# Softmax attention in a fused model kernel: 128-row score matmuls on masked operands become 32-row matmuls on slices of the transposed q and k, and the pipeline is cut into half units

## What is computed

```python
x_norm = layer_norm(x, g1, beta1)                       # inside, x is itself layer-normed once more
q, k, v = (x_norm @ W + b).reshape(B, S, H, hd)...      # B 2, S 1024, H 16, hd 8
q, k = apply_rope(q), apply_rope(k)
q = q * (1.0 / sqrt(hd))
scores = einsum('bhqd,bhkd->bhqk', q, k)
attn = softmax(scores, axis=-1)
out = einsum('bhqk,bhkd->bhqd', attn, v)
x = x + out @ Wo + bo
x = x + relu(layer_norm(x, g2, beta2) @ W1 + b1) @ W2 + b2
```

## Time and profile before

| | |
|---|---|
| median of 3 runs | 1262.15 us (1261.19 to 1263.75) |
| profiled execution, first to last instruction | 1262.4 us |
| first ring fill / first score / end of the last wave | 441.1 / 482.0 / 904.2 us |
| PE, DVE, ACT busy, share of the span | 75%, 55%, 40% |
| mean granted TensorE clock | 0.855 of full speed |

### The profile page before, as it was taken

One profiled execution on the slowest core, in us unless ns is written; L12 is line 12 of the kernel. 1 busy time (PEld: TensorE's weight loads), 2 busy tenths in 40 slices (PEclk: granted clock), 3 DMA queues, 4 the chain that ended last, 5 costly groups with the idle time before them and its releaser, 6 DMA issues.

```text
span 1262.4 us, 18479 instructions
## 1 busy us (share of the span) xinstructions
PE 947.6 (75%) x5666; PEld 520.6 (41%) x5666; DVE 693.4 (55%) x1340; ACT 506.2 (40%) x1039; POOL 250.6 (20%) x222
## 2 busy tenths in 40 slices
PE   4697637888455388899999999997877388585784
PEld 3376436666343312222222222221456366374563
DVE  6845774111379698777777777771243611466111
ACT  1110423333241604666666666666533133211332
POOL 1000043655206100000000000100020355201553
PEclk9799757988766757999999999999987588695898
DMA  6000110111300000000000000000021111101113
GB/s 174 21 1 1 67 34 23 41 41 41 88 1 0 18 17 9 1 17 17 2 17 2 17 17 0 9 1 1 8 60 67 42 41 39 44 1 34 34 41 91
DMA packets 39014, 37.12 MB, mean 29 GB/s; under 512 B 7922, under 2 KB 29762, under 8 KB 38946
## 3 DMA queue, kind: packets, MB, share of 16 engines
q1 hardware_dynamic: 33506, 25.02, 7.2%
q0 software_dynamic: 5440, 11.15, 3.3%
HBM read 22.18 MB, written 9.76 MB: 25 GB/s over the span
## 4 chain that ended last, share of the span: by engine, by line
PE 47%; DVE 22%; issue 10%; POOL 7%; ACT 4%; another core or an unknown queue 4%; DMA 3%; SPq 2%; ACTq 0%; DVEq 0%; POOLq 0%
PE psum L1333 10%; PE psum L1305 10%; PE psum L1261 7%; DVE arena L1272 6%; POOL results L887 4%; POOL arena L879 3%; DVE stats L158 2%; ACT arena L1365 2%; PE psum L912 2%; PE psum L217 2%; PE psum L930 2%; DVE xn L186 1%; PE psum L315 1%; PE psum L300 1%
## 5 line engine op out<-in xcount | busy, mean ns | idle before, releaser
L1272 DVE TENSOR_REDUCE arena<-psum 128x1 f32<-128x1024 f32 x256 | 302.6, 1221 | 93.5 <-PE psum L1261 92.2
L1365 ACT ACTIVATE arena<-psum 128x512 f32<-128x512 f32 x512 | 282.0, 595 | 179.0 <-PE psum L1333 177.7
L1261 PE MATMUL psum<-arena 128*128 128x512 f16 (+1 forms) x512 | 198.8, 411 | 14.7 <-DVE arena L1272 10.0
L1333 PE MATMUL psum<-arena 128*128 128x512 f16 x512 | 196.8, 389 | 14.5 <-ACT arena L1365 7.5
L1014 ACT ACTIVATE arena<-psum,e_b 128x128 f32<-128x128 f32 x340 | 96.4, 369 | 158.6 <-remote 127.5
L1333 PEld LDWEIGHTS psum<-arena 128*128 128x128 f16 x512 | 48.2, 97 | 221.3 <-ACT arena L1365 197.7
L1141 DVE TENSOR_TENSOR arena<-psum,arena 128x128 f32 (+1 forms) x85 | 24.8, 292 | 202.6 <-remote 149.5
L1305 PE MATMUL psum<-arena 128*32 128x512 f32 x1024 | 134.7, 604 | 0.0
L966 PE MATMUL psum<-arena,expert_w 128*128 128x128 f16 x1020 | 101.6, 240 | 33.3 <-ACT arena L1014 30.4
L977 PE MATMUL psum<-expert_w,arena 128*128 x680 | 105.7, 302 | 1.3 <-issue 0.7
L887 POOL DMA_INDIRECT results<-arena x85 | 83.6, 984 | 93.5 <-DVE arena L1141 78.0
(11 more groups left out here) (249 smaller groups left out, 1131.4 us busy)
## 6 DMA issues: line engine op xcount, KB each, us to landing
arena<-results SPq DMA_DIRECT2D x16, 256.0 KB, 3.8
arena<-arena SPq DMA_DIRECT2D x64, 64.0 KB, 2.0
tokens<-arena SPq DMA_DIRECT2D x6, 512.0 KB, 3.2
arena<-in_L_attn_b_w_dram SPq DMA_DIRECT2D x1, 2048.0 KB, 9.0
arena<-in_L_ffn_W_dram SPq DMA_DIRECT2D x1, 2048.0 KB, 8.8
arena<-tokens,arena POOLq DMA_INDIRECT x85
results<-arena POOLq DMA_INDIRECT x85
x<-in_L_attn_a_x_dram SPq DMA_DIRECT2D x2, 512.0 KB, 5.0
```

The lines of the kernel that those rows point to most:

```text
L1261: last = nc.tensor.matmul(core.psum[:, 2 * slot + half, :], self.qM[:, b, j, qt * P:(qt + 1) * P], keys, start=True, stop=True)
L1272: v.reduce_max(self.mx[:, qt, j:j + 1], core.psum[:, 2 * slot:2 * slot + 2, :].rearrange("p a n -> p (a n)"), AX.X).then_inc(self.ring_out, 1)
L1333: nc.tensor.matmul(core.psum[:, 4 + j % 2, :], self.kM[:, b, j, kt * P:(kt + 1) * P], self.qT2[:, b, 512 * half:512 * (half + 1)], start=True,
L1365: nc.scalar.activation(self.prob[:, k % 2, j, :], core.psum[:, 4 + j % 2, :], ACT.Exp).then_inc(self.prob_in, 1)
```

## The change

- `qM`, `kM`, their memsets, their 64 DMAs and POOL's value copies are gone. A fill takes 32 rows of `qT` as the stationary and 32 rows of `kT` as the moving operand; a score takes 32 rows of `kT` and of `qT2`. Head j uses rows 32j to 32j+31.
- DVE writes the projected values straight into `vs`, which now holds all heads of all tokens.
- The padding columns, `m4` and the ones are written by six ACT copies (`clear_pads`: 2048, 256, 1792, 1024, 256 and 5888 elements in each partition) between the roots of batch 0 and batch 1, and no longer by POOL. L1635's additions follow POOL's L1610 at once.
- The unit becomes a half unit of 512 queries; there are 16 (`HALVES`), unrolled. The first ring holds 17 positions. In `position`, the turn of half h stands between the second and the third fill of half h+2's maxima, no longer right behind its own last maximum. PE keeps two positions ahead of the turn (`AHEAD`).
- Scores use three banks (4, 5, 6) in rotation, `prob` has three buffers; the wave sums in bank 7 alone, and ACT, no longer DVE, copies the sum, once for each half.
- One period on PE is now: two scores, a fill (both matmuls of one head), two scores, the rest of the fills (one; in the last period of a half two, one turn among the three of that period), the wave of the period before.

```diff
-ARENA = 28608
+ARENA = 29184
...
+    HALVES = 2 * B * NG
+    POSITIONS = 17 * HALVES
+    AHEAD = 2
+    SCORE_BANKS = 3
+    PROBS = 3
...
+    def position(a):
+        if a < 17:
+            return ("turn", 0, 0) if a == 16 else ("max", 0, a)
+        if a < 33:
+            return "max", 1, a - 17
+        h, i = divmod(a - 33, 17)
+        h += 2
+        if h == SoftmaxAttention.HALVES:
+            return "turn", h - 1, 0
+        if i == 2:
+            return "turn", h - 1, 0
+        return "max", h, i - (i > 2)
...
+    def turn_at(h):
+        return 16 if h == 0 else SoftmaxAttention.POSITIONS - 1 if h == SoftmaxAttention.HALVES - 1 else 18 + 17 * h
...
     def ring_fill(self, pe, a):
+        if a >= 2:
+            pe.wait_ge(self.ring_out, a - 1)
...
-        last = nc.tensor.matmul(core.psum[:, 2 * slot + half, :], self.qM[:, b, j, qt * P:(qt + 1) * P], keys,
-                                start=True, stop=True)
+        rows = slice(32 * j, 32 * j + 32)
+        for keys in range(2):
+            k0 = b * S + 512 * keys
+            last = nc.tensor.matmul(core.psum[:, 2 * slot + keys, :], self.qT[rows, g, q0:q0 + P],
+                                    self.kT[rows, g, k0:k0 + 512], start=True, stop=True)
...
+    def score(self, pe, k, j):
+        tile = HG * k + j
+        if tile >= self.SCORE_BANKS:
+            pe.wait_ge(self.prob_in, tile - self.SCORE_BANKS + 1)
+        rows = slice(32 * j, 32 * j + 32)
+        at = b * S + kt * P
+        nc.tensor.matmul(core.psum[:, 4 + tile % self.SCORE_BANKS, :], self.kT[rows, g, at:at + P],
+                         self.qT2[rows, h % 2, :], start=True, stop=True).then_inc(self.score_in, 1)
...
     def wave(self, pe, k):
+        pe.wait_ge(self.prob_in, HG * k + HG)
+        if kt == 0 and h:
+            pe.wait_ge(self.sum_out, h)
         for j in range(HG):
+            last = nc.tensor.matmul(core.psum[32 * j:32 * j + 32, 7, :], self.vs[:, b * TB + kt, HG * g + j, :],
+                                    self.prob[:, k % self.PROBS, j, :], start=(kt == 0), stop=(kt == TB - 1))
...
+    def loop_tensor(self, pe):
+        a = 0
+        waves = TB * self.HALVES
+        for k in range(waves):
+            h, kt = divmod(k, TB)
+            upto = min(self.POSITIONS, self.turn_at(h) + 1 + self.AHEAD + (17 * kt) // TB)
+            if k == 0:
+                while a < upto:
+                    self.ring_fill(pe, a)
+                    a += 1
+            after = min(self.POSITIONS, self.turn_at(h) + 1 + self.AHEAD + (17 * (kt + 1)) // TB)
+            if kt == 0:
+                pe.wait_ge(self.ring_out, self.turn_at(h) + 1)
+            self.score(pe, k, 0)
+            self.score(pe, k, 1)
+            if a < after:
+                self.ring_fill(pe, a)
+                a += 1
+            self.score(pe, k, 2)
+            self.score(pe, k, 3)
+            while a < after:
+                self.ring_fill(pe, a)
+                a += 1
+            if k > 0:
+                self.wave(pe, k - 1)
+        self.wave(pe, waves - 1)
...
+    def loop_scalar(self, act):
+        for k in range(TB * self.HALVES):
+            h, kt = divmod(k, TB)
+            if k >= self.PROBS:
+                act.wait_ge(self.wave_in, k - self.PROBS + 1)
             for j in range(HG):
+                tile = HG * k + j
+                act.wait_ge(self.score_in, tile + 1)
+                nc.scalar.activation(self.prob[:, k % self.PROBS, j, :], core.psum[:, 4 + tile % self.SCORE_BANKS, :],
                                      ACT.Exp).then_inc(self.prob_in, 1)
+            if kt == 0 and h:
+                self.move_sum(act, h - 1)
+        self.move_sum(act, self.HALVES - 1)
...
+    def clear_pads(self, act):
+        act.wait_ge(self.w.zero_in, 3)
+        zero, shift, one = self.w.consts[:, 0:1], self.w.consts[:, 1:2], self.w.consts[:, 2:3]
+        fill(self.qs.rearrange("p t h r -> p (t h) r")[:, :, 24:32], zero)
+        fill(self.ks.rearrange("p t h r -> p (t h) r")[:, :, 24:25], shift)
+        fill(self.ks.rearrange("p t h r -> p (t h) r")[:, :, 25:32], zero)
+        fill(self.m4.rearrange("p a q n -> p (a q n)"), zero)
+        fill(self.vs.rearrange("p t h r -> p (t h) r")[:, :, 8:9], one)
+        fill(self.vs.rearrange("p t h r -> p (t h) r")[:, :, 9:32], zero)
...
     def scalar(self, act):
             deviation(core, b)
             deviation(core, b, var=5, root=6)
+            if b == 0:
+                self.clear_pads(act)
```

More of the change, by code:

```diff
@@ L1230, in __init__, with half_of @@
             self.t[b].update(x2T=core.turns(2), up=core.turns(8), down=core.turns(2))
-    RING = 34
     @staticmethod
[L1235 to L1249, removed]
+    def half_of(h):
+        b, rest = divmod(h, 2 * NG)
+        g, half = divmod(rest, 2)
+        return b, g, half
@@ L1250, in ring_fill @@
+    def ring_fill(self, pe, a):
+        core, nc, slot = self.core, self.core.nc, a % 2
+        kind, h, i = self.position(a)
+        b, g, half = self.half_of(h)
+        if a >= 2:
+            pe.wait_ge(self.ring_out, a - 1)
         if kind == "turn":
-            pe.wait_ge(self.max_in, m * 4 + (2 * b + qt + 1))
+            pe.wait_ge(self.max_in, h + 1)
             out = core.psum[:, 2 * slot, 0:256].bitcast(F16)
-            for i in range(4):
-                last = nc.tensor.transpose(out[:, i * P:(i + 1) * P], self.m4[:, 4 * qt + i, :], self.w.ident16[:, :])
+            for q in range(4):
+                last = nc.tensor.transpose(out[:, q * P:(q + 1) * P], self.m4[:, h % 2, q, :], self.w.ident16[:, :])
@@ L1304, in wave @@
+    def wave(self, pe, k):
+        core, nc = self.core, self.core.nc
+        h, kt = divmod(k, TB)
+        b, g, _ = self.half_of(h)
+        pe.wait_ge(self.prob_in, HG * k + HG)
+        if kt == 0 and h:
+            pe.wait_ge(self.sum_out, h)
         for j in range(HG):
-            last = nc.tensor.matmul(core.psum[32 * j:32 * j + 32, 6 + half, :], self.vs[:, b, kt, j, :],
-                                    self.prob[:, k % 2, j, :], start=(kt == 0), stop=(kt == TB - 1))
+            last = nc.tensor.matmul(core.psum[32 * j:32 * j + 32, 7, :], self.vs[:, b * TB + kt, HG * g + j, :],
+                                    self.prob[:, k % self.PROBS, j, :], start=(kt == 0), stop=(kt == TB - 1))
@@ L1450, in tensor, with fill @@
                 last.then_inc(core.filled[turn.bank], 1)
+    def clear_pads(self, act):
+        core, nc = self.core, self.core.nc
+        def fill(out, what):
+            shape, src = list(out.shape), what
+            for _ in range(len(shape) - 2):
+                src = src.unsqueeze(2)
+            nc.scalar.copy(out, src.to_broadcast(shape)).then_inc(self.pads, 1)
+        act.wait_ge(self.w.zero_in, 3)
[6 more added lines that the diff above has]
+        fill(self.vs.rearrange("p t h r -> p (t h) r")[:, :, 9:32], zero)
     def scalar(self, act):
@@ L1474, in scalar @@
                                ps[:, turn.bank, :].bitcast(F16)).then_inc(core.emptied[turn.bank], 1)
-        for b in range(B):
-            self.unit_scalar(act, b, 0)
-        with act.Fori(1, NG) as g:
-            for b in range(B):
-                self.unit_scalar(act, b, g)
+        self.loop_scalar(act)
         for b in range(B):
```

244 lines of the change are left out of this document (60 added, 184 removed).

## The result

The changed kernel takes 1379.85 us (median of 4 runs, 1378.02 to 1381.54) where the kernel before, timed again beside it, takes 1262.72: 1.0936 times as long, 95% interval 1.0917 to 1.0954. The forecast was 1177 us with a range of 1145 to 1228. The rival with the clock, in its variant with overlap, said 1393.

What follows compares the result with a forecast made beforehand. PE was taken to set the pace, with the bank wait and the turn on top. From 1262.4 us, 81 less in the attention and 4 less ahead of the rings gave 1177.5, forecast as 1177; range 1145 to 1228.

Steps and rivals of the forecast that it cites:

- The rival with the clock: Attention loop stays at 1.2 GHz because 32-row matmuls count less: 1526 us, or 1393 with overlap; chance 0.12.
- Bank wait: Third score's wait for the first Exp, with two score banks: 0.27 us a period, gone with three.
- Overlap: Scores and fills on different strips: period 2.83 us without overlap, mean 2.71 with full overlap in order; 2.77 taken.
- ACT's copy of the sum: In the next half's first period, after its four Exps: delays the next Exp, costing 0.3 us a half.
- Weight loads: Rival: 32-row loads no longer hide beside matmuls, 0.32 us a matmul, 3.63 a period, 1280 us; chance 0.06.
- Turn: DVE's last maximum, scaling, transposes and addition with PE idle: 1.8 us a half falls to about 0.
- Behind the first half: After half 0, four fills stand in one period, which DVE paces: a surcharge of 2.0 us.
- First ring: Before the first score: 16 maxima and one turn instead of 32 and two; first score at 462.9 us.
- Last half: The final half, without fills: 2.40 us a period, 19.2 in all, and 0.4 for the end.
- Ahead of the rings: Before the attention: POOL's memsets go, ACT clears instead, DVE's additions end earlier; gain 4 us, bounds 0 to 10.

Runs made afterwards that it cites:

- a_rows128: The changed kernel with masked queries, so that scores and fills take 128 rows; 1173.30 us, 0.9606 of the kernel before the change.
- a_warm: The changed kernel with 60 full 128-row matmuls put ahead of the first score; 1353.31 us, one run.
- a_onestrip: The changed kernel with all heads' scores and fills taken from rows 0 to 31, so none overlap; 1507.16 us, one run.
- a_rows64: The changed kernel with masked queries and strips of 64 rows for scores and fills; 1164.31 us, 0.9537 of the kernel before the change.
- a_rows64_fills: The changed kernel with masked queries on 64-row strips and the fills' heads in the order 2, 0, 3, 1; 1156.21 us, 0.9466 of the kernel before.
- a_scores128: The changed kernel with masked scores over 128 rows and fills left on 32 rows; 1208.51 us, 0.9893 of the kernel before the change.

## Why the prediction was wrong

**The step that failed** is the weighing of the clock rival, given 0.12: "Against it: the new period has PE issuing nearly all the time, and it rose at once when PE was busy 5.00 of 5 us". PE was busy 552.4 of 560.7 us and the clock stayed at 0.50. In the rows cited PE worked on 128 rows; the change alters just that, so those rows said nothing of the new work. The pair of rows named ahead of that sentence was the better sign: 81% busy with 128-row work at 1.00, and 79% in the first ring, also of 128 rows, at 0.51, so busy time alone didn't sort them. By the runs it is the height of the scores and fills: 1222, 1245 and 1391 us for one program at 128, 64 and 32 rows; not the new order (a_rows128 at 1.00), not where the clock starts (a_warm), not the overlap (a_onestrip). Why the chip grants less for such work is not shown; only that it does.

The Trainium skill, "TensorE: Matmul & The Clock Gate", Part 1 (What's actually happening), says that the clock follows how busy PE has been. Taken as the profile's busy time, a_onestrip, with PE busy 50.00 of 50 us at 0.50, does not bear it out.

**The mechanism behind the clock** was sized well by the rival: 4.5 us a period and 1393 in all, measured 4.39 (4.60 and 4.19 in turn) and 1380; a half takes 34.8 us (the waves' 552.9 us over 127 periods, times 8) for its 36. Overlap gave a little more than assumed.

**The rest of the change**, read in a_rows128 and a_rows64, worked:

- *Bank wait*: gone. Between the second and the third score PE has work, and the period without overlap is 2.89 us for the 2.83 forecast; the fourth score comes 1.14 us after the first, not 1.08.
- *Overlap*: real, and stronger than "in order". In a_rows64_fills a period is 2.67, between the 2.60 and the 2.77 of the forecast. At 32 rows it exists, but never at the high clock for a whole loop.
- *ACT's copy of the sum*: 0.14 us a half in a_rows128 (the period with it is 3.03 or 3.02 us, the others 2.89), forecast 0.3.
- *Weight loads*, a rival with 0.06: they don't stand in the open. In a_onestrip each load follows a matmul on its own strip, and pairs of starts still lie 0.43 us apart (607.41, 607.84, 608.27), what 512 columns cost at this clock.
- *Turn*: with one addition (the change as made) its period is 4.60 us, the same as others of those two heads, so it costs nothing, as forecast, but at half the clock and with overlap. Without overlap it costs 0.64 (a_onestrip, 6.03 for 5.39), and at the high clock with masks 1.27, of which 0.44 aren't the masks'.
- *Behind the first half*, with four fills in one period: 4.3 us in a_rows128 (periods of 3.68 and 6.44 for two of 2.89), the masked turn's 1.27 in it, and 3.4 in the changed kernel (5.18 and 6.96 for 4.61 and 4.18); forecast 2.0. This term was too small.
- *First ring*: 21.4 us from the first fill to the first score (457.99); forecast 21.8 (441.1 to 462.9), measured before 40.9.
- *Last half*: 2.46 us a period in a_rows128, forecast 2.40.
- *Ahead of the rings*: 2.5 us, forecast 4. The timeline of the changed kernel, which answers to the earlier trace rows:

```profile
376.69 5.52 ACT L1465 CAST arena<-consts 128x2048 f16<-128x2048 f32 x4
...
381.60 1.78 DVE L168 TENSOR_SCALAR ln_small<-ln_small 128x8 f32<-128x8 f32 x1
...
382.12 5.53 ACT L1465 COPY arena<-consts 128x256 f32<-128x256 f32 x2
...
387.55 0.29 ACT L209 ACTIVATE ln_small<-ln_small,eps 128x8 f32<-128x8 f32 x1
387.87 0.20 DVE L179 RECIPROCAL ln_small<-ln_small 128x8 f32<-128x8 f32 x1 [4.23 <-ACT ln_small L209]
...
389.29 2.14 DVE L186 TENSOR_SCALAR arena<-x,ln_small 128x128 f32<-128x128 f32 x8
389.63 8.45 PE L1395 MATMUL psum<-sa_wqkv,xnT 128*128 128x384 f32 x16 [8.20 <-ACT xnT L1488]
...
395.52 4.68 POOL L1620 TENSOR_TENSOR xn<-xn,sa_bo 128x1024 f32<-128x1024 f32 x2
...
398.65 2.64 DVE L1552 TENSOR_TENSOR arena<-expert_w,rope 128x1024 f32<-128x1024 f32 x1
```

DVE's short scaling at 381.60 takes 1.78 us beside POOL's arithmetic and the wait for the root hides it, as forecast. ACT's clears take 11.0 us for 10.4 forecast, DVE waits 4.23 for the root behind them, and the scaling of batch 1 is 2.14 us instead of 8.83, all in the way forecast. The additions end at 398.65, 400.65 on the old trace's time (the stage began 2.0 earlier), for 399.4 forecast: 0.4 late from the clears (387.6 + 2.0 for 389.2) and 0.9 from PE's 16 projections, 8.45 us instead of 7.53. Then the rotation's first multiplication takes 2.64 us instead of 1.21, with POOL's moved additions beside it (395.52 to 400.20): 1.4 us, which the forecast named as at most 1.5 and left out of the sum. Of these 2.7 us some 1.2 came back before the first fill; where was not followed.

Had the clock held, the time would likely have come out inside the forecast's range, though somewhat above its 1177. No run shows 32 rows at the high clock; the nearest is a_rows64, with the same order, clock 1.00 and overlap, 4.6% below before, where the forecast was 6.7% and its range 2.7% to 9.3%. Its four additions stand for one in each of 15 turns, at most 1.28 us each (1.70 less 0.42); without them it is, as an estimate, at most 6.2% below. a_rows128, without overlap, is 3.9% below. Its half takes 24.52 us (six periods of 2.89, one of 3.02, one of 4.16) where 22.9 were forecast without overlap: 1.27 of the turn and 0.06 for each of eight periods, less what ACT's copy saved.

## What to carry to other kernels

Cutting a matmul's rows from 128 to 32 saved nothing in the old order and can cost half of TensorE's clock for the whole loop: time one loop with the shorter operands alone, and look at the granted clock before building a pipeline on it. Rows of zeros kept the clock here; where strips should overlap, 64 rows did both here. A row is evidence for a clock only if PE does in it the work that the new loop does; busy time isn't that.

## What the runs showed of the hardware

- PE at 1.2 GHz though busy 50.00 of 50 us, with scores and fills on 32 rows (a_onestrip); within 6 us of 32-row work the clock fell from 1.00 to 0.50 (a_warm). With half of these matmuls on 128 rows it rose from 0.50 to 1.00 (a_scores128, at 464 us).
- Matmuls on a free strip start ahead of ones that stand earlier in the program. In a_rows64 the order is score, score, fill; the fill on the other strip starts at 600.82, the second score at 601.03. The Trainium skill, "TensorE: Matmul & The Clock Gate", Part 3 (The mechanism), says that matmuls start in strict program order; this trace does not bear that out for different strips.
- A switch between 32-row and 128-row matmuls costs 0.10 us each way (a_scores128).
